# A graph network's one-hot loop: its preparation spread differently over GpSimd, ScalarE and VectorE

## The reference

```python
z = edge_attr_3 @ conf_w.T + conf_b          # 20000 logits
weight = sigmoid(z)                          # 1 / (1 + exp(-z))
counts[s, d] = number of edges s -> d        # 640 x 640
W[s, d]      = sum of weight over edges s -> d
```

## Time and profile before

| | |
|---|---|
| median of 3 runs | 1647.14 us (1646.83 to 1648.19) |
| profiled execution | 1645.13 us |
| its span in the trace | 1643.5 us |
| granted TensorE clock, mean | 0.992 |
| busy share: PE, DVE, ACT, POOL | 95%, 72%, 67%, 41% |
| `front`'s preparation and prologue | 0 to 22.75 us |
| its one-hot loop | 22.75 to about 105 us |

### The profile page before, as it was taken

How to read it: one execution, slowest core, us unless ns; L and a number is a source line. 1 busy time by engine, 2 the same in 40 slices (tenths; PEclk the granted TensorE clock), 3 DMA queues, 4 the chain that set the end, 5 groups by cost and what they waited for, 6 DMA issues and landing times. The chain is left out here.

```text
span 1643.5 us, 24989 instructions
## 1 busy us (share of the span) xinstructions
PE 1557.3 (95%) x8530; PEld 1218.5 (74%) x8530; DVE 1189.6 (72%) x1896; ACT 1102.0 (67%) x1534; POOL 677.4 (41%) x498
## 2 busy tenths in 40 slices
PE   5889899999999999999999999999999999999987
PEld 4765586888788778877854777777777777777874
DVE  8977656556465646475723599888898888889877
ACT  9841545544554546454530699999999999999963
POOL 3410200120012001200302788788888888888601
PEclk9999899999999999999999999999999999999989
DMA  3001320012012200212007867777777777777710
GB/s 106 0 20 66 96 78 27 28 58 87 22 33 84 77 1 33 84 33 90 28 3 232 160 142 151 144 149 147 145 150 145 150 147 148 146 148 149 172 39 32
DMA packets 107046, 153.94 MB, mean 94 GB/s; under 512 B 42042, under 2 KB 47034, under 8 KB 106466
## 3 DMA queue, kind: packets, MB, share of 16 engines
q0 software_dynamic: 72832, 87.84, 28.1%
q1 hardware_dynamic: 34146, 65.21, 12.5%
HBM read 141.02 MB, written 11.73 MB: 93 GB/s over the span
## 5 line engine op out<-in xcount | busy, mean ns | idle before, releaser
L1772 POOL DMA_INDIRECT edge_gathered<-dst_table,edge_index x158 | 266.4, 1686 | 58.7 <-issue 53.6
L223 PE MATMUL edge_z2p<-edge_w_hi,edge_h_hi 128*128 128x512 f32 x628 | 256.6, 409 | 1.7 <-DVE edge_late L2095 1.7
L223 PE MATMUL edge_z2p<-edge_w_hi,edge_h_lo 128*128 128x512 f32 x628 | 248.6, 396 | 0.0
L223 PE MATMUL edge_z2p<-edge_w_lo,edge_h_hi 128*128 128x512 f32 x628 | 248.3, 395 | 0.0
L1741 POOL DMA_INDIRECT edge_gathered<-src_table,edge_index x158 | 201.6, 1276 | 85.4 <-POOL edge_index L1735 30.6
L973 POOL TENSOR_TENSOR h<-h,tr_row_b 128x512 f32<-128x512 f32 x40 | 59.2, 1513 | 274.2 <-ACT C L1213 273.8
L962 POOL TENSOR_TENSOR tr_cw<-w_c,tr_cw 32x1024 fp32r<-32x1024 f32 x7 | 16.6, 2376 | 346.1 <-ACT tr_cw L1173 346.1
L223 PEld LDWEIGHTS edge_z2p<-edge_w_hi,edge_h_hi 128*128 128x128 f32 x628 | 117.9, 188 | 54.9 <-issue 29.8
L223 PEld LDWEIGHTS edge_z2p<-edge_w_hi,edge_h_lo 128*128 128x128 f32 x628 | 118.1, 188 | 28.7
L223 PEld LDWEIGHTS edge_z2p<-edge_w_lo,edge_h_hi 128*128 128x128 f32 x628 | 118.1, 188 | 24.7
L2095 DVE TENSOR_TENSOR edge_late<-edge_z2p,w_c 128x1024 f32<-128x1024 f32 x79 | 96.7, 1224 | 44.9 <-PE edge_z2p L223 44.6
(11 more groups left out here) (364 smaller groups left out, 4019.9 us busy)
## 6 DMA issues: line engine op xcount, KB each, us to landing
w_c<-in_attr_T SPq DMA_DIRECT2D x78, 128.0 KB, 4.1
agg<-edge_sum_rows POOLq DMA_DIRECT2D x36, 128.0 KB, 10.6
w_a<-in_wv SPq DMA_DIRECT2D x4, 1024.0 KB, 5.3
w_b<-in_wq SPq DMA_DIRECT2D x4, 1024.0 KB, 5.5
w_a<-in_wk SPq DMA_DIRECT2D x4, 1024.0 KB, 7.8
w_b<-in_wo SPq DMA_DIRECT2D x4, 1024.0 KB, 7.1
w_a<-in_m SPq DMA_DIRECT2D x4, 1024.0 KB, 5.4
w_b<-in_m SPq DMA_DIRECT2D x4, 1024.0 KB, 5.3
```

Source lines behind the costliest of these rows:

```text
L223: mm = pe.matmul(out, a, b, start=(n == 0), stop=(n == last))
L1772: pool.indirect_dma_start(out=from_rows[ring][:, j, :].bitcast(F32), out_offset=None, in_=k.dst_table, in_offset=bass.IndirectOffsetOnAxis ...
```

## The change

The zeroing of `sums` moves from ACT to POOL, as five memsets right behind the identity matrix. ACT makes the weights: the exponential as before, then, once DVE has bounded it and added 1, the logarithm, the exponential of its negative, and the scaled high part as f16. DVE does the bounding and adding ahead of the window table, and after it only the low part. In the prologue the destination comparisons of two groups now stand ahead of their source comparisons; before, the source comparisons of groups 0 and 1 stood first of all.

```diff
--- before.py
+++ after.py
@@ -44,6 +44,7 @@
 EATTR = 64
 EPS = 1e-5
 NONE = -1.0e30
+LARGE = 1.0e18
 LOG_AND_EXP = "natural_log_exp_and_others"
 CAP = 20.0
 
@@ -248,7 +249,6 @@
         attr3, confb = sb("attr3", [P, TILES, 3]), sb("confb", [P, 4])
         wz, wr = sb("wz", [P, TILES]), sb("wr", [P, TILES])
         wb = sb("wb", [P, TILES, 2], F16)
-        wf = sb("wf", [P, TILES])
         from_onehot = [k.w_c[:, :, :].rearrange("p a b -> p (a b)").bitcast(F16)[:, 0:TPG * NP].rearrange(
             "p (t n) -> p t n", n=NP)] + [sb(f"from_onehot{a}", [P, TPG, NP], F16) for a in range(1, RING)]
         to_onehot = [sb(f"to_onehot{a}", [P, TPG, 3, WIN], F16) for a in range(RING)]
@@ -339,6 +339,8 @@
                 pool.wait_ge(ident_zero, 1)
                 pool.affine_select(out=k.ident[:, :], in_=k.ident[:, :], compare_op=ALU.not_equal, fill=1.0,
                                    base=0, pattern=[[-1, P]], channel_multiplier=1).then_inc(ident_made, 1)
+                for i in range(NT):
+                    pool.memset(sums[:, i, :, :], 0.0).then_inc(sums_zero, 1)
                 n = sweeps(pool)
                 with pool.Fori(0, n * (GROUPS // RING) + GROUPS // RING) as t:
                     for a in range(RING):
@@ -354,13 +356,14 @@
             def _(act):
                 act.preload_act_table_set(LOG_AND_EXP)
                 own = Count(act, sca)
-                act.wait_ge(ident_made, 1)
-                for i in range(NT):
-                    if i == 3:
-                        act.wait_ge(z_ready, 1)
-                        act.activation(wz[:, :], wz[:, :], ACT.Exp, scale=-1.0).then_inc(exp_ready, 1)
-                    act.activation(sums[:, i, :, :].rearrange("p a b -> p (a b)"), k.ident[:, 0:1].to_broadcast([P, 3 * WIDE]),
-                                   ACT.Copy, scale=0.0).then_inc(sums_zero, 1)
+                act.wait_ge(z_ready, 1)
+                act.activation(wz[:, :], wz[:, :], ACT.Exp, scale=-1.0).then_inc(exp_ready, 1)
+                act.wait_ge(z_ready, 2)
+                own(act.activation(wr[:, :], wz[:, :], ACT.Ln))
+                own.wait()
+                own(act.activation(wr[:, :], wr[:, :], ACT.Exp, scale=-1.0))
+                own.wait()
+                act.activation(wb[:, :, 0], wr[:, :], ACT.Copy, scale=SCALE_HI).then_inc(exp_ready, 1)
                 act.wait_ge(inputs_ready, 3)
 
                 def last_tile(u, a):
@@ -569,6 +572,8 @@
                 own(dve.tensor_reduce(shared[:, 0, :], cols(ps_row[:, 0, :], SHARE), AX.X, ALU.min))
                 step(dve.tensor_reduce(shared[:, 1, :], cols(ps_row[:, 1, :], SHARE), AX.X, ALU.max))
                 step(dve.tensor_tensor(shared[:, 1, :], shared[:, 1, :], shared[:, 0, :], ALU.subtract))
+                dve.wait_ge(exp_ready, 1)
+                dve.tensor_scalar(wz[:, :], wz[:, :], LARGE, 1.0, ALU.min, ALU.add).then_inc(z_ready, 1)
                 for w in range(MAXSWEEPS):
                     own(dve.tensor_scalar(cols(wtab[:, w * GROUPS:(w + 1) * GROUPS], SHARE),
                                           shared[:, 0, :, None].to_broadcast([1, SPANS, SHARE]), float(WIN * w),
@@ -580,14 +585,8 @@
                 dve.tensor_copy(k.starts[:, :], wtab[:, :]).then_inc(windows_known, 1)
                 dve.tensor_copy(k.sweeps[:, :], span1[:, 1:2]).then_inc(windows_known, 1)
 
-                dve.wait_ge(exp_ready, 1)
-                step(dve.tensor_scalar(wz[:, :], wz[:, :], 1.0, None, ALU.add))
-                step(dve.reciprocal(wr[:, :], wz[:, :]))
-
-                step(dve.tensor_scalar(wr[:, :], wr[:, :], 0.0, SCALE_HI, ALU.max, ALU.mult))
-                step(dve.tensor_copy(wb[:, :, 0], wr[:, :]))
-                step(dve.tensor_copy(wf[:, :], wb[:, :, 0]))
-                step(dve.tensor_tensor(wr[:, :], wr[:, :], wf[:, :], ALU.subtract))
+                dve.wait_ge(exp_ready, 2)
+                step(dve.scalar_tensor_tensor(wr[:, :], wr[:, :], SCALE_HI, wb[:, :, 0], ALU.mult, ALU.subtract))
                 step(dve.tensor_scalar(wb[:, :, 1], wr[:, :], SCALE_LO, None, ALU.mult))
 
                 def start_of(u):
@@ -610,15 +609,13 @@
                     ins.then_inc(from_ready, 1)
 
                 dve.wait_ge(inputs_ready, 3)
-                for a in range(SHARE):
-                    compare_from(a, a)
                 n = sweeps(dve)
                 for a in range(0, RING, SHARE):
                     start = start_of(a)
                     for b in range(SHARE):
                         compare_to(a + b, a + b, start)
-                for a in range(SHARE, RING):
-                    compare_from(a, a)
+                    for b in range(SHARE):
+                        compare_from(a + b, a + b)
                 dve.wait_ge(sums_zero, NT)
 
                 def add_span(s, a, start):
```

## The result

The changed kernel takes 1653.80 us (median of 8 runs, 1651.04 to 1656.38), against 1647.41 us for the kernel before (8 runs). The ratio is 1.0038, with a 95% interval from 1.0029 to 1.0047: it is slower by 6.4 us, and the interval lies above 0.2%. The forecast was 1652.8 us. The size was right, and the largest term of the sum came about in another way than the one I had put first: as the first rival, whose sum was 1654.6 us. The medians can't tell these two apart (1.0 and 0.8 us off); the profile can.

A forecast was written before the change was run, and what follows sets the result against it. The loop runs at DVE's pace, so preparation counts by shifting the loop's start: +6.4 us for memsets holding casts in turns, -0.75 for weights and order, +5.65 on 1647.14 gives 1652.8 us; range 1645.8 to 1655.5.

The forecast's parts named there:

- the largest term of the sum: Preparation: POOL's five memsets take turns with DVE's casts and tensor_scalars, L561 starting at about 12.55 instead of 6.14; +6.4 us.
- the first rival: Preparation: POOL keeps its turn through five memsets, first cast waits until about 11.6; +7.5 us, 1654.6 us; chance 0.17.
- The edge weights: Preparation: seven DVE instructions go, 0.95 us comes back, ACT's activations cost nothing; weights ready at 10.85 instead of 12.87, -2.0 us.
- Destination comparisons first: Prologue: register loads bare on DVE, 1.4 us; source comparisons take turns with POOL's weightings; with the weights, -0.75 us.
- PE's 6.04 us for two groups: Loop's start: time from PE's first matmul until two groups are done, carried over unchanged, slow first group included.
- The memset's length: POOL's zeroing of sums: 1.87 us for each memset of 2112 elements, five taking 9.4 us, from 2.34 to 11.7.
- A memset holds a cast: Preparation: POOL's memset fully stops DVE's casts and tensor_scalars, not the reductions; cost lies between nothing and a full stop.
- Turns: Preparation: after each POOL memset one waiting DVE cast runs, then the next memset; +6.4 us there, +5.65 in all; chance 0.50.
- POOL keeping its turn: Preparation: memsets without waits between them hold L548 until about 11.6, +8.2 us, less 0.75: +7.5 us; chance 0.17.
- The case that it stays the same: Whole kernel: no measurable change, from memsets that don't hold DVE, except where all extra gains come together; chance 0.27.
- no hold: Preparation: memsets don't hold DVE, only -0.75 us stays, 1646.4 us, no measurable change; chance 0.25.

The follow-up runs named there:

- the two-input run: Changed kernel with the first cast written as a two-input tensor_tensor maximum of the rows with themselves; 1652.80 us against 1647.34 for the kernel before, ratio 1.0037.
- the run with 55 extra matmuls: Kernel before with weights alone changed, ACT's last zeroing pieces between its first tiles, 55 unread PE matmuls ahead of the loop; 1653.72 us, ratio 1.0045.

## Why the prediction was right, and where a step of it was not

**The edge weights: right.** Forecast -2.0 us; from the end of the first cast to the end of the weights it is 7.06 us instead of 9.17, -2.1. ACT's three activations end at 17.42, before DVE has the window table (18.14), so they cost nothing, as reckoned.

**Destination comparisons first: right, with misses that nearly cancel.** Forecast: 1.4 us bare for the register loads (1.65 measured), PE 3.65 us behind the first destination comparison (3.35), the loop 9.7 us behind it (9.92). The last holds a term that was carried over without a reason, PE's 6.04 us for two groups: it came as 6.57 here, and as 5.06 to 6.43 in the other runs where PE had been idle before. All of it together with the weights was to give -0.75 us; measured in the changed kernel it is 7.49 - 7.95 = -0.46, and -0.99 at PE's first matmul (6.96 - 7.95). The order alone costs 1.3 to 1.5 us at the loop's start, where the sum had 1.25 (2.0 - 0.75), and its run shows both mechanisms in its rows: 1.65 us of idle time, and three source comparisons in 2.54 us.

**The memset's length: right.** 1.87 us forecast from two short ones, 1.85 measured for each; five take 9.05 us, back to back.

**A memset holds a cast: right, and shown.** That was the disputed cost, between nothing and a full stop. The run with the memsets alone has the whole loss (+8.02 at the loop's start); without them the kernel is as fast as before (1.0001); and the two-input run separates what is held from what is not. The rule of the Trainium skill (SBUF — State Buffer, section "Who interferes with whom"), that an instruction with both ports on one input and a GpSimd instruction shut each other out while a two-input one is held only by a GpSimd instruction that reads, agrees with that run: 0.68 us for the two-input maximum beside a memset, 6.65 us for the cast behind it.

**Turns: wrong.** "With turns, as in the prologue" is the step that failed. I gave them 0.50 and POOL keeping its turn 0.17, which came: +8.2 forecast for it at the first cast, 7.95 measured; +7.5 at the loop's start, 7.49 measured. That the last agrees to 0.01 us is luck: the hold was 0.25 us shorter than that sum and the rest of the change gained 0.29 us less. The difference between the two is whether POOL's next instruction is already queued: with a wait between the memsets, the forecast turns appear one for one, with L561's counterpart at 12.24 us (12.55 forecast) and the loop at 27.99 (28.4 forecast). The prologue, from which I drew the turns, has such gaps: POOL does register operations of 0.09 to 0.14 us before each weighting. That these gaps are what let DVE in there is my reading; only the memsets were tested with and without a gap. The row that showed the other case, the comparison that waited for weighting 5, I had put among the rivals.

**The median came out at 1652.8 + 1.0 all the same,** because the median moved 6.4 us where the loop's start moved 7.49; the sum had 5.65 for both. So the nearness of the total is in part luck. The interval of the ratio, 4.8 to 7.7 us, holds both numbers. The scatter behind the loop (3.8 us in the transformer, 3.0 us in the edge layer, over these profiles) is enough for that. The granted clock at one such place is shown above; that all of the scatter is the clock's is only argued.

**Chances and range.** The case that it stays the same had 0.27, nearly all of it on memsets that don't hold DVE; they do. The range of 1645.8 to 1655.5 was drawn for turns and for no hold; that it also takes in the case that came (1654.6 by its sum, 1653.80 measured) was not its purpose.

## What to carry to other kernels

Work given to an idle POOL is not free when DVE's path runs casts beside it (memsets, +8.0 us) or tensor_scalars (weightings, 2.54 us for three instead of 0.98): look at what DVE does at that time, and if POOL's long instructions must run there, try a wait between them, which brought the loop 2.3 us forward here. Where instructions are reordered in a prologue, look at what ran over the register loads, since they come bare when the queue ahead of them is empty. And where a gain is smaller than the scatter behind it, as the 2.6 us here, read it at the landmark, say that the total doesn't show it, and take the landmark apart: 1.0 of the 2.6 us was another engine's pace.

## What the runs showed of the hardware that I had not expected

A cast that waits for POOL is passed over as long as POOL's next instruction is already queued: five memsets of 1.85 us or fifteen of 0.68 held it for 8.4 to 9.0 us in all. A wait on a semaphore between them, 0.06 us in POOL's records, ends that. Reductions and the two-input maximum beside the memsets take 0.67 to 0.68 us and are not held.

PE's first 20 one-hot matmuls take 1.81 or 1.82 us in the three runs where PE worked just before them, and 3.16 to 3.38 in all the other profiles. The view of stretches gives the same granted clock for both, here for the slow ones of the kernel before:

```profile
16.70:18.70 2.00, 1.99 (x13) 1.89 (x14) 2.00 (x3) 1.97 (x5) 2.00 (x2) 1.00 0.19 70
```

13 matmuls in 2 us, where the same loop later starts 27 at the same 1.00. So which of the two levels this stretch had can't be read from that column, and that the slow matmuls are the lower level is my guess from their pace. Two groups from PE's start took 3.7 us where PE had worked before, and 5.1 to 6.6 us where it had not; why these differ by 1.5 us, no run tells. (The run with 55 extra matmuls, where the two groups waited for ACT, is left out of this.)
